# Order of the bias fills and engine of the far copies in a disentangled attention stage

## The reference

```python
scores = einsum('bhsd,bhkd->bhsk', q, k) / sqrt(hd * 3)
c2p = einsum('bhsd,hkd->bhsk', q, pos_k)      # then taken at clip(rel + span)
p2c = einsum('bhsd,hkd->bhsk', k, pos_q)      # then taken at clip(-rel + span), transposed
scores = scores + c2p / bias_scale + p2c / bias_scale
probs = softmax(scores)
ctx = einsum('bhsk,bhkd->bhsd', probs, v)
```

## Time and profile before

| | |
|---|---|
| time, median of 3 runs | 1401.23 us (1401.13 to 1408.01) |
| time of the profiled execution | 1402.82 us |
| span in its profile | 1401.0 us |
| mean granted clock of TensorE over the span | 0.865 |
| busy share of TensorE, VectorE, ScalarE, GpSimd | 77%, 64%, 50%, 33% |

### The profile page before, as it was taken

How to read it: one execution, slowest core, us unless ns; L and a number is a source line. 1 busy time by engine, 2 the same in 40 slices (tenths; PEclk the granted TensorE clock), 3 DMA queues, 4 the chain that set the end, 5 groups by cost and what they waited for, 6 DMA issues and landing times. The chain is left out here.

```text
span 1401.0 us, 34774 instructions
## 1 busy us (share of the span) xinstructions
PE 1080.8 (77%) x9380; PEld 853.3 (61%) x9380; DVE 902.8 (64%) x3061; ACT 695.8 (50%) x1691; POOL 458.2 (33%) x506
## 2 busy tenths in 40 slices
PE   4892616784717999999999999999999999743786
PEld 3792505773416676767676767767676767542676
DVE  6887654566625666666767676766666678562555
ACT  2236302442625565666666565656566665311343
POOL 2404133752203233323323232323232333004764
PEclk9996557997857999999999999999999999855999
DMA  5910142323362212122121212121211110032431
GB/s 146 222 25 0 57 154 86 117 84 76 109 227 70 66 50 59 52 52 59 43 61 46 65 47 65 47 64 47 62 49 57 55 52 8 1 136 78 115 97 46
DMA packets 83508, 103.23 MB, mean 74 GB/s; under 512 B 16473, under 2 KB 71200, under 8 KB 82944
## 3 DMA queue, kind: packets, MB, share of 16 engines
q1 hardware_dynamic: 77824, 89.92, 23.6%
q0 software_dynamic: 5632, 12.70, 2.6%
HBM read 67.86 MB, written 35.74 MB: 74 GB/s over the span
## 5 line engine op out<-in xcount | busy, mean ns | idle before, releaser
L1230 POOL TENSOR_SCALAR ds_scores<-ds_scores,ds_max 128x256 f32<-128x256 f32 x256 | 236.3, 923 | 511.7 <-DVE ds_max L1463 511.6
L1455 DVE TENSOR_TENSOR ds_p2c<-ds_bank,ds_p2c 128x512 f32<-128x512 f32 x256 | 175.6, 686 | 154.9 <-PE ds_bank L1289 154.8
L1402 ACT ACTIVATE all_xt<-ds_bank 128x512 f32<-128x512 f32 x256 | 152.9, 597 | 105.7 <-PE ds_bank L1307 99.4
L1463 DVE CUSTOM_DVE_ANT_0 ds_scores<-ds_bank,ds_p2c 128x256 f32<-128x256 f32 x512 | 197.0, 422 | 0.2 <-DVE ds_p2c L1455 0.2
L1289 PE MATMUL ds_bank<-all_constants,ds_c2p_t 128*128 128x128 f32 x1024 | 174.3, 297 | 0.0
L1307 PE MATMUL ds_bank<-all_constants,ds_scores 128*128 128x128 f32 x1024 | 160.3, 280 | 1.9 <-ACT all_xt L1402 1.6
L1289 PEld LDWEIGHTS ds_bank<-all_constants,ds_c2p_t 128*128 128x128 f32 x1024 | 125.0, 150 | 48.0 <-issue 35.6
L1307 PEld LDWEIGHTS ds_bank<-all_constants,ds_scores 128*128 128x128 f32 x1024 | 125.9, 146 | 8.0 <-issue 1.8
L1385 ACT ACTIVATE ds_c2p_t<-ds_bank 128x256 f32<-128x256 f32 x256 | 77.6, 390 | 60.3 <-PE ds_bank L1280 60.3
L1296 PE MATMUL ds_bank<-ds_ks,ds_qs 72*128 72x256 bf16 x512 | 103.1, 284 | 1.4 <-DVE ds_max L1463 1.4
L1280 PE MATMUL ds_bank<-d_qr,ds_tab 64*128 64x128 f32 x1024 | 79.3, 297 | 30.1 <-DMA ds_tab<-scratch_tables 28.1
(11 more groups left out here) (285 smaller groups left out, 2010.8 us busy)
## 6 DMA issues: line engine op xcount, KB each, us to landing
ds_tab<-scratch_tables SPq DMA_DIRECT2D x64, 248.0 KB, 3.5
slots_in<-all_zero SPq DMA_DIRECT2D x2, 5180.0 KB, 38.0
ds_qs<-scratch_q_parts SPq DMA_DIRECT2D x32, 288.0 KB
ds_ks<-scratch_k_parts SPq DMA_DIRECT2D x96, 96.0 KB
d_qr<-scratch_qk SPq DMA_DIRECT2D x512, 4.0 KB
d_kr<-scratch_qk SPq DMA_DIRECT2D x512, 4.0 KB
0fe_xb<-slots_in SPq DMA_DIRECT2D x40, 129.5 KB, 2.1
1fe_xb<-slots_in SPq DMA_DIRECT2D x40, 129.5 KB, 2.2
```

The lines of the kernel that those rows point to most:

```text
L1230: pool.tensor_scalar(S[b % NS][:, 1, :], S[b % NS][:, 1, :], mx[:, 2 * b + 1:2 * b + 2], None, ALU.subtract).then_inc(s_sub1, 1)
L1402: act.activation(PT[b], pt2[:, :].rearrange("p (k s) -> p k s", k=2), ACT.Exp).then_inc(s_exp, 1)
L1455: dve.tensor_tensor(z, pt1[b % 2][:, :].rearrange("p (a k) -> p a k", a=2), z, ALU.add).then_inc(s_z, 1)
L1463: last = dve.tensor_tensor_reduce(out=S[b % NS][:, st, :], in0=pqk[b % 2][:, st * SEQ:(st + 1) * SEQ], in1=PC[half][:, st, b, :], scale=1. ...
```

## The change

The order of the fills becomes, step by step: pair; pair; pair (kind 1); far and edge; far and near, which completes kind 0; pair (kind 1); far and near; far and edge, all of kind 1. The far outputs of kind 0 are copied by ScalarE, those of kind 1 still by VectorE, so that `BA` becomes 14 and `BD` 2. TensorE does `av` ahead of the fills of its step. At the start of a unit it waits for one copy, that of the near fill of kind 0.

```diff
-        FILLS = [PAIRS[0][0], PAIRS[0][1], PAIRS[1][0], PAIRS[1][1], NEAR[0], NEAR[1],
-                 FARS[0][0], EDGE[0], FARS[0][1], FARS[1][0], EDGE[1], FARS[1][1]]
+        FILLS = [PAIRS[0][0], PAIRS[0][1], PAIRS[1][0], FARS[0][0], EDGE[0], FARS[0][1], NEAR[0],
+                 PAIRS[1][1], FARS[1][0], NEAR[1], FARS[1][1], EDGE[1]]
...
-        BY_DVE = [f[0] == "far" for f, banks in zip(FILLS, BANKS) for _ in range(banks)]
+        BY_DVE = [f[:2] == ("far", 1) for f, banks in zip(FILLS, BANKS) for _ in range(banks)]
...
-        SHARE = [1, 1, 1, 1, 1, 2, 2, 3]
+        SHARE = [1, 1, 1, 2, 2, 1, 2, 2]
...
-                    for item in (FIRST[FILLS.index(EDGE[0])], FIRST[FILLS.index(FARS[0][1])]):
+                    for item in (FIRST[FILLS.index(NEAR[0])],):
                         copied(pe, head, half, item)
...
                             t2(*before)
+                        if n % 4 == 3 and (before := group_before(head, half, n, 7)):
+                            av(*before)
                         if not (last and half == 1):
                             for _ in range(SHARE[n]):
                                 fill(*following(head, half), done)
                                 done += 1
-                        if n % 4 == 3 and (before := group_before(head, half, n, 7)):
-                            av(*before)
...
                 if what == "far":
+                    if kind == 0:
+                        side, quad = where
+                        act.wait_ge(s_bm, done + 1)
+                        act.activation(to[:, side, :, quad * 64:(quad + 1) * 64], pb[FIRST[n] % 2][:, :].rearrange("p (b s) -> p b s", b=HALF),
+                                       ACT.Copy).then_inc(s_be, 1)
                     return
...
-                if what == "far":
+                if what == "far" and kind == 1:
```

## The result

The changed kernel takes 1327.84 us (median of 4 runs, 1326.92 to 1330.51) against 1404.23 us (1401.13 to 1408.01; 4 runs, one more than the table of before has): a ratio of 0.9458, 95% interval 0.9424 to 0.9492, or 76 us less. The forecast was 1320 with a range of 1305 to 1345. The profiled execution took 1330.51 us, its span is 1328.7; the span of before was 1401.0, so 72.3 us are to be found in the two traces.

What follows compares the result with a forecast made beforehand. TensorE's pace was taken as the bound, with a gap and low clock in each unit. Savings of 81 (30 units) + 1 + 1 - 1 = 82 us from 1402.82 gave 1320.8, stated as 1320, range 1305 to 1345.

Steps and rivals of the forecast that it cites:

- The 1.58 us gap: In step 7, TensorE waited 1.58 us each unit for VectorE's far copy; low clock behind it cost 1.45 us.
- The walk through a unit: Step-by-step pricing of one changed unit at full clock, checking whether each fill finds its bank copied: 21.2 us.
- The three waits: New TensorE waits for ScalarE's copies: 0.17 us in step 0, 0.08 in step 4, 0.25 in step 5.
- The clock: TensorE's clock in the units, 0.93 before, was taken as full, 1.00, since the new waits are short.
- SyncE's whole train: SyncE's DMA issues for a unit: 20.7 us, a floor under the 21.2 us unit with 0.5 to spare.
- rival (b): SyncE's issue train stretches by a microsecond and becomes the bound: units of 21.9 us, total 1341; chance 0.04.
- The landing: Arrival of the loaded parts that step 3's far fill needs: about 5 us into the unit, 4.7 early.
- rival (d): Parts land late for step 3's far, so TensorE stands still each unit: slower, 1479 us at worst; chance 0.02.
- the first unit and its surroundings: First unit of the stage: loses its 1.6 us gap, less 0.4 of new waits; 1 us gained.
- the fills before it: Fills before the first unit, with nothing to hide a copy: one more 1.2 us copy between fills; 1 us lost.
- the last unit: The stage's last unit, without fills, no longer starts at the low clock: about 1 us gained.
- The ring: The chain of fills and copies over two banks in each unit, put at 21.2 us.

Runs made afterwards that it cites:

- one_copy: The kernel before with only the first far output of kind 1 copied by ScalarE instead of VectorE: 1329.16 us, ratio 0.9459.

## Why the prediction was right, point by point

**What bound the kernel.** Right. The 1.58 us gap and the low clock behind it were the two parts of the loss. One moved copy, without any new order, brings both back.

**The walk through a unit.** Right within 0.2 us: 21.2 forecast, 21.04 in a unit without a DMA wait. The three waits were put at 0.17, 0.08 and 0.25; they are 0.19, 0.03 (far to near is 0.35, 769.53 to 769.88, against 0.32) and 0.12. The two far fills directly behind t2 start 0.1 earlier than assumed. In return, the walk priced every far at 0.32, but the two of before that stood directly in front of a t1 took 0.23 (836.89 to 837.12), and in the new order none stands there. ScalarE's copy of 128x512 takes 0.60, as put.

**The clock.** Right: 1.00 over 28 units, but for the one unit of 24.46. The rule cited from the Trainium skill ("TensorE: Matmul & The Clock Gate", A second HAM failure mode: psum-queue depth-cycling), that many short waits on a ring of banks can let the clock swing, has no case here: short waits of 0.03 to 0.52 us left it at 2.4 GHz, in the changed kernel and in one_copy.

**SyncE.** Here is the step that failed: "SyncE's whole train takes 20.7 us ... At a unit of 21.2 it still fits, with 0.5 to spare". The term was mis-sized. The 20.7 run from the first issue to the end of the last; between two trains that follow without a pause lie 0.36 and 0.78 us more, in turn, and the rate is 42.73 / 2 = 21.37 us. So rival (b), given 0.04, is what sets the pace, only at 21.4 and not at 21.9, as the experiments with more issues and with the tables on GpSimd show. It costs 30 x (21.36 - 21.04) = 10 us.

The landing was mis-sized too. It was put at T+5, 4.5 us after the first issue, from a DMA share that was "down to 0.17" in the half microsecond from 774.5. But 0.17 is hardly less than the 0.20 of the whole stretch, so it shows no end of a transfer. In the same trace the share rises to 1.01 in the half microsecond from 776.0 and is down only at 777.5, the first table being in this too; the semaphore events put the last landing of the parts at 776.3, 6.3 us after the first issue:

```profile
776.00:776.50 0.50, 0.50 (x7) 0.47 (x6) 0.32 (x2) 0.50 (x4) 0.50 (x1) 1.00 1.01 56
776.50:777.00 0.50, 0.50 (x6) 0.34 (x4) 0.50 (x2) 0.50 (x3) 0.21 (x1) 1.00 0.77 302
777.50:778.00 0.50, 0.50 (x13) 0.48 (x10) 0.50 (x3) 0.22 (x1) 0.00 (x0) 1.00 0.04 8
```

So with the train on time the slack was 3.6 us at the median landing and 1.6 at the latest, not 4.7. The train falls behind the units by 0.3 us each time, and where it has fallen behind and a late landing comes on top, TensorE waits: seven waits of 0.17 to 1.88 us. One of them brought the clock down, in the unit of 24.46: 21.04 + 1.88 + 1.54. The mechanism of rival (d), parts needed before they land, thus exists at a small size.

**The rest of the sum.** In the profiled executions: the 30 units 76.6 us less (forecast 81), the first unit and its surroundings 1.1 (1), the fills before it 1.4 lost (1 lost), the last unit 0.3 lost (1 gained), 0.2 lost before the stage, and 3.4 lost behind it, where the code is the same. The forecast had nothing for these 3.4. TensorE's first rows there are at half the clock (2.79 us for 12 transposes, 1.50 before), and so is `av` at the end of the last unit (1.93 at 1119.10, where it took 1.07 before at 1195.99). This goes with the order of the fills: the six kernels with the new order on this chip show 2.79 and took 203.5 to 208.2 us behind the stage, the four with the old order 1.50 and 201.8 to 203.0, and on the other chip it is 2.79 against 1.50 as well. Why the clock falls there, in a unit that has no fills, stays open.

The number is closer than its terms. The ring came out 4.8 us better than put, 30 x (21.2 - 21.04), SyncE's train took 10 back, and the last unit and what is behind the stage, together put at 1 gained, lost 3.7.

## What to carry to other kernels

When a short fill waits for its bank, look at which queue the copy of the fill before stands in and what is ahead of it there; swapping that one copy to the engine that is free, or putting the next long piece of work between the two, is worth as much as a new order. Price the gap with what TensorE's clock loses behind it, since here that was as much again. And before a loop gets shorter, compare every periodic chain in it with the new period from start to start, the DMA issues of a queue too. What lay 2.5 us under the loop became its bound at once, and since the far fills now need their loads two steps earlier, its lateness turned into waits.

## What the runs showed of the hardware

Whether the clock falls behind a wait of TensorE is not decided by the wait alone. Waits of 0.03 to 0.66 us in each unit left it at 1.00 in four kernels, and 1.58 in each unit lowered it in 28 of 30. Between and above, the traces show both: in the changed kernel 1.31 and 1.65 did not lower it and 1.88 did; with more issues 1.52 did and 1.83 did not; with `av` behind 2.05 did and 2.24 did not. These are the units of 1.52, 1.83 and 2.24:

```profile
1044.78:1068.88 24.10, 22.41 (x222) 17.06 (x221) 15.36 (x55) 16.21 (x37) 7.38 (x9) 0.93 0.20 55
704.55:727.47 22.92, 20.87 (x222) 15.84 (x220) 15.36 (x55) 16.11 (x37) 7.37 (x9) 1.00 0.20 57
936.39:959.29 22.90, 20.61 (x225) 15.80 (x221) 15.35 (x55) 16.21 (x38) 7.41 (x9) 1.00 0.27 58
```

Fewer DMA issues are not a faster transfer. Three loads of 96 KB as one of 288 KB saved 0.5 us of issuing (1.26 to 0.77) and landed some 3 us later (9.4 against 6.3 in the median); in the form written here only 3 of its packets were in flight at a time, where there had been 12.

GpSimd issued the two loads in 0.68 and 0.62 us, against 0.8 each on SyncE, and its own shifts kept their 0.92 us.
